# A graph layer with a mixture-of-experts layer behind it: the routing of tokens to experts rewritten

## Time and profile before

| | us |
|---|---|
| median of three runs | 2161.12 (2155.4 to 2163.2) |
| the profiled execution: time | 2156.78 |
| its span | 2155.1 |
| residual stage | about 1551 to 1717.6 |
| routing stage | 1717.6 to 1746.7 |
| expert stage | 1747.3 to 2155 |

### The profile page before, as it was taken

One profiled execution on the slowest core, in us unless ns is written; L12 is line 12 of the kernel. 1 busy time (PEld: TensorE's weight loads), 2 busy tenths in 40 slices (PEclk: granted clock), 3 DMA queues, 4 the chain that ended last, 5 costly groups with the idle time before them and its releaser, 6 DMA issues. The chain is left out here.

```text
span 2155.1 us, 28177 instructions
## 1 busy us (share of the span) xinstructions
PE 2020.4 (94%) x9449; PEld 1606.9 (75%) x9449; DVE 1283.1 (60%) x2385; ACT 971.9 (45%) x1519; POOL 947.0 (44%) x837
## 2 busy tenths in 40 slices
PE   7999999999999999999989999999799769899984
PEld 6777787777777777777768677677478558788863
DVE  7589878842222222218999988888788742121367
ACT  3211122222222222218999989999744313233352
POOL 0000036555555556408777778878400012222364
PEclk9999999999999999999999999999999969999997
DMA  5322277777777778769789989989666589999775
GB/s 185 103 80 78 81 239 257 262 248 262 258 255 254 252 250 261 241 191 320 257 301 311 320 271 336 348 300 320 243 218 212 175 315 329 292 344 342 233 198 108
DMA packets 158843, 530.74 MB, mean 246 GB/s; under 512 B 32698, under 2 KB 33082, under 8 KB 156506
## 3 DMA queue, kind: packets, MB, share of 16 engines
q1 hardware_dynamic: 83706, 308.63, 41.1%
q0 software_dynamic: 75008, 220.50, 33.3%
HBM read 396.38 MB, written 163.47 MB: 260 GB/s over the span
## 5 line engine op out<-in xcount | busy, mean ns | idle before, releaser
L216 PE MATMUL psum<-w_hi,xnT_hi 128*128 128x512 f32 (+1 forms) x1592 | 420.8, 399 | 10.1 <-issue 5.0
L216 PE MATMUL psum<-w_lo,xnT_hi 128*128 128x512 f32 (+1 forms) x1592 | 419.9, 395 | 0.0
L216 PE MATMUL psum<-w_hi,xnT_lo 128*128 128x512 f32 (+1 forms) x1592 | 413.0, 394 | 0.0
L585 ACT ACTIVATE work<-psum 128x512 f32<-128x512 f32 (+1 forms) x150 | 89.7, 598 | 674.1 <-PE psum L216 674.1
L919 POOL DMA_INDIRECT sorted_rows<-acc x313 | 339.0, 1083 | 116.4 <-issue 83.6
L216 PEld LDWEIGHTS psum<-w_hi,xnT_hi 128*128 128x128 f32 (+1 forms) x1592 | 292.9, 187 | 81.0 <-issue 9.3
L216 PEld LDWEIGHTS psum<-w_lo,xnT_hi 128*128 128x128 f32 (+1 forms) x1592 | 295.7, 186 | 74.4
L216 PEld LDWEIGHTS psum<-w_hi,xnT_lo 128*128 128x128 f32 (+1 forms) x1592 | 294.7, 185 | 71.9
L1035 POOL DMA_INDIRECT w_hi<-y_rows,sort_row x168 | 228.7, 1362 | 64.9 <-issue 39.2
L1035 POOL DMA_INDIRECT w_lo<-y_rows,sort_row x164 | 216.7, 1321 | 61.2 <-issue 42.3
L1120 DVE SCALAR_TENSOR_TENSOR w_hi<-w_hi,sort_recip,y_hi 128x1024 fp32r<-128x1024 f32 x168 | 213.8, 1283 | 38.5 <-ACT y_hi L1081 34.0
(11 more groups left out here) (371 smaller groups left out, 2701.3 us busy)
## 6 DMA issues: line engine op xcount, KB each, us to landing
split_experts<-acc SPq DMA_DIRECT2D x128, 512.0 KB
ring<-split_experts SPq DMA_DIRECT2D x16, 4096.0 KB, 16.1
w_raw<-in_wchunks SPq DMA_DIRECT2D x86, 512.0 KB, 5.2
y_rows<-work SPq DMA_DIRECT2D x144, 256.0 KB, 2.8
acc<-in_wchunks SPq DMA_DIRECT2D x64, 512.0 KB, 5.9
work<-local_rows SPq DMA_DIRECT2D x26, 384.0 KB, 4.3
acc<-in_bias SPq DMA_DIRECT2D x10, 512.0 KB, 5.5
sorted_rows<-acc POOLq DMA_INDIRECT x313, 4.9
```

The costliest lines, as they stand in the source:

```text
L216: i = pe.matmul(to[:rm, :], x_[:, k, m * P:m * P + rm], w_[:, s, k * HALF:(k + 1) * HALF], start=(n == 0), stop=(n == 3 * KD - 1))
L585: act.activation(stage_y[:rows(m), t % 4, :], bank[t % 4][:rows(m), :], ACT.Copy)\
```

## The change

Residual stage:

- The router weights' high and low parts stand side by side (`wr_pair`, 16 columns). A tile's logits are 16 matmuls: the stationary operand is now the slice of 128 tokens, the moving operand the 16 columns (with the tokens' high part, then with their low part). The result has tokens on partitions, and ACT copies 16 numbers per token to `lg_raw`. The low-by-low product comes in besides. The final transposes and copies go.
- The turn of the last tile goes to banks 0 and 1 and waits for the gate product's read there, not for the low part of the tile before.
- POOL makes the constants at the start of this stage. Behind the last tile DVE adds bias and the low half, and picks the two largest: for each, a maximum, equality, a weight that falls with the index, a second maximum, equality. PE makes the two counting matmuls here, the triangle now filled with -1 so that one sum later gives the place. `chosen` is laid out expert by column. The stage ends after the counts.

Routing stage:

- One scan over 160 numbers (a `resume` operand restarts it at each expert) reads the counts in PSUM directly, in place of two copies and 8 scans; the two additions of the prefix become one.
- `hot_high` and `hot_token` come before `hot_low`, which is written in four quarters, each of 5 columns; PE starts its 20 list matmuls on the first.
- What only the expert stage needs (softmax weights, `past`, `expert_of`, `bias_at` and what follows from them) is behind; `token_at` is made right after the list, from 2 steps and one more, and `row_at` in one instruction in place of seven.

Its core:

```diff
-        wr_hi = sb("wr_hi", [P, KD, E], F32R)
-        wr_lo = sb("wr_lo", [P, KD, E], F32R)
+        wr_pair = sb("wr_pair", [P, KD, 2 * E], F32R)
+        wr_hi, wr_lo = wr_pair[:, :, 0:E], wr_pair[:, :, E:2 * E]
...
+        chosen = w_raw[:, 0, 0:E * COLS].rearrange("p (e c) -> p e c", e=E)
+        lane_f, top, low, token_f = w_raw[:, 1, 0:P], w_raw[:, 1, P:P + 16], w_raw[:, 1, P + 16:P + 32], w_raw[:, 1, P + 32:P + 48]
+        top, low, token_f = top[:, 0:TILES], low[:, 0:TILES], token_f[:, 0:TILES]
+        part_f, valid = w_raw[:, 1, P + 48:P + 49], w_raw[:, 1, P + 49:P + 50]
...
+            def turned(m):
+
+                return 6 if m < TILES - 1 else 0
...
-                        act.activation(lgT[:, (s - 2) * P:(s - 2) * P + rows(s - 2)], bank[4][:E, 0:rows(s - 2)],
-                                       ACT.Copy).then_inc(lg_out, 1)
+                        act.activation(lg_raw[:rows(s - 2), s - 2, :], bank[4][:rows(s - 2), 0:2 * E], ACT.Copy).then_inc(lg_out, 1)
...
-                act.wait_ge(lg_rows, 1)
-                act.activation(router[:, 0:TILES - 1, :].rearrange("p m e -> p (m e)"),
-                               bank[0][:, 0:(TILES - 1) * E], ACT.Copy)
-                act.activation(router[:rows(TILES - 1), TILES - 1, :],
-                               bank[0][:rows(TILES - 1), (TILES - 1) * E:TILES * E], ACT.Copy)
...
+                pool.memset(r_tri[:, :], 0.0).then_inc(made, 1)
+                pool.memset(r_ones[:, :], 1.0).then_inc(made, 1)
+                pool.iota(lane_i[:, :], pattern=[[1, P]], base=0, channel_multiplier=0).then_inc(made, 1)
+                pool.iota(token_i[:, :], pattern=[[P, TILES]], base=1, channel_multiplier=1).then_inc(made, 1)
+                pool.iota(part_i[:, :], pattern=[[0, 1]], base=0, channel_multiplier=1).then_inc(made, 1)
+                pool.iota(worth_i[:, :], pattern=[[-1, E]], base=E, channel_multiplier=0).then_inc(made, 1)
+                pool.wait_ge(made, 6)
+                pool.affine_select(out=r_tri[:, :], in_=r_tri[:, :], compare_op=ALU.is_gt, fill=-1.0, base=0,
+                                   pattern=[[1, P]], channel_multiplier=-1).then_inc(made, 1)
...
+                        if s == TILES:
+                            pe.wait_ge(z_read, TILES - 1)
+                        elif s - 2 >= 0:
                             pe.wait_ge(tlo, 2 * (s - 1))
-                        transposed(s - 1, 6, tT_done)
+                        transposed(s - 1, turned(s - 1), tT_done)
...
-                        for w_, x_ in ((wr_hi, opT_hi), (wr_lo, opT_hi), (wr_hi, opT_lo)):
+                        for x_ in (opT_hi, opT_lo):
                             for k in range(KD):
-                                i = pe.matmul(bank[4][:E, 0:rows(m)], w_[:, k, :], x_[:, k, m * P:m * P + rows(m)],
-                                              start=(n == 0), stop=(n == 3 * KD - 1))
+                                i = pe.matmul(bank[4][:rows(m), 0:2 * E], x_[:, k, m * P:m * P + rows(m)], wr_pair[:, k, :],
+                                              start=(n == 0), stop=(n == 2 * KD - 1))
...
-                pe.wait_ge(lg_out, TILES)
-                pe.wait_ge(z_read, TILES)
-                for m in range(TILES):
-                    i = transpose(pe, bank[0][:rows(m), m * E:(m + 1) * E], lgT[:, m * P:m * P + rows(m)], E)
-                i.then_inc(lg_rows, 1)
+                pe.wait_ge(made, 7)
+                pe.wait_ge(chosen_ready, 2)
+                flat = chosen[:, :, :].rearrange("p e c -> p (e c)")
+                pe.matmul(bank[0][:, 0:COLS * E], r_tri[:, :], flat, start=True, stop=True)
+                pe.matmul(bank[1][:, 0:COLS * E], r_ones[:, :], flat, start=True, stop=True).then_inc(counted, 1)
...
+                for at, need in ((slice(0, TILES - 1), TILES - 1), (slice(TILES - 1, TILES), TILES)):
+                    v.wait_ge(lg_out, need)
+                    n = at.stop - at.start
+                    link(v.tensor_tensor(lg[:, at, :], lg_raw[:, at, 0:E], br_bc[:, :].unsqueeze(1).to_broadcast([P, n, E]), ALU.add))
+                    link(v.tensor_tensor(lg[:, at, :], lg[:, at, :], lg_raw[:, at, E:2 * E], ALU.add))
+                weighed = worth[:, :].unsqueeze(1).to_broadcast(three_d)
+                for k in range(2):
+                    most = low if k else top
+                    link(v.reduce_max(most[:, :], lg, axis=AX.X))
+                    link(v.tensor_tensor(equal[:, :, :], lg, most[:, :].unsqueeze(2).to_broadcast(three_d), ALU.is_equal))
+                    link(v.tensor_tensor(ranked[:, :, :], equal[:, :, :], weighed, ALU.mult))
+                    link(v.reduce_max(best[:, :], ranked[:, :, :], axis=AX.X))
+                    picked = chosen[:, :, k * TILES:(k + 1) * TILES]
+                    link(v.tensor_tensor(picked.rearrange("p e t -> p t e"), ranked[:, :, :],
+                                         best[:, :].unsqueeze(2).to_broadcast(three_d), ALU.is_equal))
+                    if k == 0:
+                        link(v.scalar_tensor_tensor(out=lg, in0=picked.rearrange("p e t -> p t e"), scalar=-3e38, in1=lg,
+                                                    op0=ALU.mult, op1=ALU.add))
+                    at = chosen[:, :, (k + 1) * TILES - 1]
+                    v.tensor_scalar(at, at, valid[:, 0:1], None, ALU.mult).then_inc(chosen_ready, 1)
+                v.tensor_tensor(low[:, :], low[:, :], top[:, :], ALU.subtract)
...
+                pool.memset(resume[:, :, :], 1.0).then_inc(made, 1)
+                pool.wait_ge(made, 8)
+                pool.memset(resume[:, :, 0:1], 0.0).then_inc(made, 1)
                 pool.memset(t_s[:, :, :], 0.0).then_inc(made, 1)
-                pool.wait_ge(made, 8)
+                pool.wait_ge(made, 10)
                 pool.wait_ge(token_ready, 1)
...
+                    if c % PART_C == 0:
+                        pe.wait_ge(hot_ready, c // PART_C + 1)
...
+                v.tensor_scalar(spare_row[:, :], token_f[:, 0:1], float(N + 1), None, ALU.add)
+                v.wait_ge(made, 9)
                 v.wait_ge(counted, 1)
-                v.tensor_copy(prefix[:, :, :].rearrange("p c e -> p (c e)"), bank[0][:, 0:COLS * E])
-                link(v.tensor_copy(total[:, :, :].rearrange("p c e -> p (c e)"), bank[1][:, 0:COLS * E]))
-                for e in range(E):
-                    i = v.tensor_tensor_scan(running[:, e, :], ones_c[:, :], total[:, :, e], 0.0, ALU.mult, ALU.add)
-                link(i)
-
+                link(v.tensor_tensor_scan(running[:, :, :].rearrange("p e c -> p (e c)"), resume[:, :, :].rearrange("p e c -> p (e c)"),
+                                          bank[1][:, 0:COLS * E], 0.0, ALU.mult, ALU.add))
                 link(v.tensor_scalar(blocks_f[:, :], running[:, :, COLS - 1], float(BLOCK_T - 1), None, ALU.add))
+                v.tensor_tensor(prefix[:, :, :].rearrange("p e c -> p (e c)"), running[:, :, :].rearrange("p e c -> p (e c)"),
+                                bank[0][:, 0:COLS * E], ALU.add)
...
-                v.tensor_tensor(prefix[:, :, :], prefix[:, :, :], total[:, :, :], ALU.subtract)
+                link(v.tensor_tensor_scan(block_end[:, :], ones_c[:, :], blocks_f[:, :], 0.0, ALU.mult, ALU.add))
                 link(v.tensor_tensor(start[:, :], block_end[:, :], blocks_f[:, :], ALU.subtract))
-                link(v.tensor_tensor(past[:, :, :], lane_f[:, 0:BLOCKS_T].unsqueeze(2).to_broadcast([P, BLOCKS_T, E - 1]),
-                                     start[:, 1:E].unsqueeze(1).to_broadcast([P, BLOCKS_T, E - 1]), ALU.is_ge))
-                link(v.reduce_sum(listed[:, 0:BLOCKS_T], past[:, :, :], axis=AX.X))
-                v.tensor_copy(expert_of[:, :], listed[:, 0:BLOCKS_T])
-                v.tensor_scalar(bias_at[:, :], listed[:, 0:BLOCKS_T], part_f[:, 0:1], None, ALU.is_equal)
-                link(v.tensor_tensor(prefix[:, :, :], prefix[:, :, :], running[:, :, :].rearrange("p e c -> p c e"), ALU.add))
...
+                for q in range(4):
+                    at = slice(q * PART_C, (q + 1) * PART_C)
+                    v.tensor_tensor(hot_low[:, at, :], lane_f[:, :].unsqueeze(1).to_broadcast([P, PART_C, P]),
+                                    low_f[:, at].unsqueeze(2).to_broadcast([P, PART_C, P]), ALU.is_equal).then_inc(hot_ready, 1)
+                v.wait_ge(exp_out, 1)
+                link(v.tensor_scalar(top[:, :], ex[:, :], 1.0, None, ALU.add))
+                link(v.reciprocal(weight_of[:, 0, :], top[:, :]))
+                link(v.tensor_tensor(weight_of[:, 1, :], ex[:, :], weight_of[:, 0, :], ALU.mult))
...
+                v.wait_ge(list_done, 1)
+                v.tensor_scalar(empty[:, :], bank[2][:, 0:TILES_T], 0.0, None, ALU.is_equal)
+                link(v.tensor_scalar(tokens[:, :], bank[2][:, 0:TILES_T], -1.0, None, ALU.add))
+                v.scalar_tensor_tensor(out=token_at[:, :], in0=empty[:, :], scalar=float(Y_PAD), in1=tokens[:, :],
```

(65 more changed lines are left out.)

72 lines of the change are left out of this document (19 added, 53 removed).

## The result

The changed kernel takes 2165.06 us (median of 19 runs, 2157.92 to 2173.99) against 2160.69 for the kernel before on the same chips: ratio 1.003, 95% interval 1.0018 to 1.0042. The forecast was 2155.6, so the sign is wrong: the way from the routing stage's entry to the first tokens did become 6.2 us shorter, but the end of the residual stage before it 5.7 us longer, and the logits in the loop cost 7.4 us more where about 2 had been forecast. The profiled execution took 2161.87 us with a span of 2160.1, 5.0 longer than the span before, and shows both.

The account below looks back on a forecast made before the run. The expert stage, at TensorE's pace, was taken to begin with the first token gather's landing: -5.9 us there plus 2.4 for logits gives -3.5, put on the four-run mean 2159.1: 2155.6 us, range 2147.5 to 2165.

Parts of the forecast that it names:

- The starting point: Expert stage runs at TensorE's pace from the first token gather's landing; whatever moves its begin (1749.39) moves the end.
- Step 1: Residual loop: 16 new logit matmuls at 0.13 us each cost +0.35 us a tile, +2.4 us over seven tiles.
- Step 2: End of residual stage: last turn 1.2 us earlier, ranking moved in; routing entered at 1721.5 instead of 1717.6.
- Step 3: Routing stage: shorter chain makes `token_ready` 12.3 us behind the entry, at 1733.8 instead of 1743.59, 9.8 us earlier.
- Step 4: First token gather shares DMA with the second weight half, landing at 1743.5, 5.9 us earlier than before, not 9.8.
- The gather is not held: Rival, chance 0.22: first token gather lands as if alone, at 1739.6; -7.4 us, 2151.7 us.
- Given back in the expert stage: Rival, chance 0.16: expert stage's waits for gathers, 5.5 us together, may double; +2 us, 2161 us.
- The slower rival: Chance 0.12: logits in the residual loop cost 0.22 us a matmul, +1.7 us a tile; +5.7 us, 2164.8 us.

Follow-up runs that it names:

- e1: Changed kernel with the old logits (24 matmuls, final transposes and router copies) back, the rest of the change kept; 2153.74 us, 0.998 of the kernel before.
- e2: Changed kernel with the 16 router-weight columns streamed eight times over (128 moving columns), same loads; 2160.06 us, 1.0005 of the kernel before.
- e3: Kernel before with the new logits alone, one DVE addition replacing final transposes and router copies, old routing; 2171.0 us, 1.0049 of the kernel before.
- e6: Changed kernel with 20 unread 512-column matmuls while TensorE waits for the last tile's rows; 2160.83 us, 1.0013 of the kernel before.
- e5: Changed kernel with POOL's clear of the token buffers held until the first quarter of `hot_low` is made; 2165.78 us, 1.0031 of the kernel before.
- e4: Changed kernel with the second weight half issued only when the first token gather has landed; 2173.57 us, 1.0061 of the kernel before.
- h1: Changed kernel with old logits, constants, ranking and counting matmuls moved behind the stage boundary, and POOL's clear held; 2150.2 us, 0.9964 of the kernel before.

## Why the prediction was wrong

**The starting point was right.** What moved the first turn of tokens moved the end: of the +5.0 us of the span, the expert stage gives -1.6, which is less than the 8 us by which its length scatters between the profiles.

**Step 1 failed, with the largest share.** Of the 8.5 us missed, 5.3 are its own; steps 2 and 4 together missed 5.4, so either part alone would have left the span within half a microsecond of the one before. e1 and e2 bear that out: without the new logits the kernel is a little faster than before (0.998), with them and without the fall of the clock no different (1.0005). The matmuls' own price was even a little high: 0.112 us from start to start, not 0.13, sixteen in 1.8, and a tile period without a fall of the clock is 15.12 (1601.57 to 1616.69), +0.17 and not +0.35. The 0.13 came from a reading: it divides the 1.06 us of eight turnings by eight, and these 1.06 include the end of the last one. From start to start give 0.82 (1645.91 to 1646.73), 0.10 each, and by duration the logits' 1.04 us equal the turning's 1.06. The Trainium skill ("TensorE: Matmul & The Clock Gate", section "LDWEIGHTS (loading the stationary operand)") gives a load's time as its columns divided by 1.2, in ns, 107 for 128 columns; at full clock this trace agrees within 5%, with 0.112 us for a logit matmul. The step fails at what it took for granted, that TensorE keeps "this clock" behind the new matmuls. Sixteen 128-column loads with 16 moving columns each show as busy in the records (2.57 of 3 us of loads in the window from 1613), and yet the clock granted behind them is the lower level for some three microseconds in four of the six tiles: the first eight gate matmuls 3.66, 3.43, 3.06 and 3.51 us where it is 2.09 at full clock. That makes the periods 1.6 us longer for each fall on average (two whole ones are 16.70 and 16.67 against 15.12), 6.4 in all. With +0.17 six times that makes the measured +7.4. The cost falls on instructions that the change doesn't touch, so no price per matmul could hold it. e1 and e3 put it on this edit, e2 on the few moving columns and not on the loads. In each of the five profiles with these logits two of the six tiles are spared, and not always the same ones; why stays open.

**Step 2 was mis-sized, for the same reason.** The earlier turn came, 0.06 us behind the end of the last normalisation (1716.18 against 1715.31 + 0.81). From it to the entry I had 12.4 us and there are 14.28. Tile 8's logits take 3.59 us to their copy (1717.54 to 1721.13), where the sum had 2.6, and tile 9's, with their copies and the wait, 3.35 more where it had 2.65: both run at the lower level, 0.21 us a matmul from start to start for tile 8's, and the sum had mixed 0.13 and 0.22. The ranking takes 4.2 us instead of 3.7; the turn and the counting matmuls were 0.3 shorter than forecast. e6 brings tile 8's logits to 1.96 us and the whole stretch to 12.65. (The sum's 1721.2 for the counts is 0.2 more than its own 1719.6 + 1.4.)

**Step 3 was right**: `token_ready` 12.8 us behind the entry, forecast 12.3. The scan took 0.49, forecast 0.45. The delay under POOL's clear came, in one instruction, `blocks_f`: 1.20 us, ending with the clear (1731.42 + 1.20 and 1730.80 + 1.80, within 0.02), 0.17 with the clear moved (e5), so 1.0 and not 0.7. The scan, which reads PSUM, ran beside the same clear unharmed. The delay cost nothing that can be seen in the time, for the reason in step 4.

**Step 4: the mechanism was right, the size was not.** The gather meets the weights and is held by them (e4 takes the second half away: 4.5 us; in e5 an earlier start brings nothing). But it took 11.5 us from issue to the turn, not 8.4; the first turn came 25.5 behind the entry, forecast 22.0. The landings of the two weight halves and then of the first two gathers in the changed kernel show where the term was short:

```profile
L1486 SPq DMA_DIRECT2D ring<-split_experts x2: 360/394/427, 1730.5 to 1730.9; - x2
...
DMA to landing us min/median/max: 12.2/17.7/23.3
```

```profile
DMA to landing us min/median/max: 11.0/11.2/11.4
```

I had the halves through 20.4 us behind the entry, from windows of two levels of DMA share. The second half lands 23.3 us after an issue at 1730.9, at 1754.2, which is 23.7 behind the entry: 3.3 of the 3.5 us missed. The gather lands at 1755.9 (11.4 after 1744.52), 1.7 later, where the sum had 1.6. In the earlier trace rows the second half had 21.3 to its landing, at 1739.3, 1.3 us after the traffic of the earlier trace rows had ended, so 20.4 was short from the start; the 2.0 more fit three gathers of 512 KB among the weights where the sum counted one, which is argued and not shown. The term also scatters with this routing: from the entry to the first turn 25.5 us in the profiles of the changed kernel, e2 and e5, 24.3 in e6, 23.1 in e1. It scatters with the weights: their second half lands 23.7, 23.6, 24.4, 23.0 and 22.2 us behind the entry, in that order, and the first gather 0.9 to 1.9 us after it in all five. So e1's tokens came sooner because its weights did; why the weights' own time varies stays open. By the rule of the Trainium skill ("DMA: Bandwidth & Descriptors", section "Queues, rings and completion order") the gather was estimated to land at 1741, 19.5 us behind the forecast entry; all five profiles are farther from it than from my sum, and the measurement decides.

**The rivals.** "The gather is not held" is wrong. "Given back in the expert stage" is not seen (404.1 us against 405.7). The slower rival has the right place, the logits in the loop, and nearly the right time (2164.8 against 2165.06), but by the wrong mechanism: at full clock the price per matmul is 0.112. The upper end of the range, 2165.0, came from it. Its price, had it been true, would have come with the forecast -9.8 from the entry to the tokens and +3.9 for the two rows before; measured are -6.2 and +5.7, and +7.4 in the loop in place of its +11.6, so that the near agreement is chance.

## What to carry to other kernels

A matmul with few moving columns can cost time after itself: before such a run is put among full-width ones, look at the granted clock behind the nearest like stretch, and compare the instructions that follow, not only those added. When work is moved across a point at which another queue issues large loads, count it against those loads too: ranking ahead of the boundary delayed 8 MB of weights, and with the ranking behind it (h1 against e1) the first tokens came 4.9 us earlier in one profile of each, of which the time shows 3.5 us by the medians, with intervals that overlap. A clock or a landing that the sum takes for granted deserves a rival of its own.

## What the runs showed of the hardware

Matmuls of 16 moving columns and matmuls of 128 with the same 128-column load cost nearly the same by themselves (1.04 and 1.09 us for eight), while the granted clock in the four microseconds behind them falls in four of six tiles with the one (to 0.59 behind the first of them; the same count in each of five profiles), and is 1.00 throughout with the other. Widening the moving operand to eight times its columns thus made the six tiles 6.0 us shorter (95.52 to 89.48). And at the lower level the same eight logits take 1.85 us, 1.8 times as long, though the load moves as many bytes. A gather of 512 KB that meets the second of two 4 MB loads lands with it: in five profiles it takes 9.0 to 12.4 us from its issue and lands 0.9 to 1.9 us behind that load; in e4, where the second load waits for it, it takes 4.5 us.
